# Score units in pairs of their own place, and two engines' SBUF operations ordered apart, in a decoder layer on one core

## Chip, cores, metric

One core of one Trainium2 chip. The metric is the device time of one launch in microseconds (us); lower is better. The kernel is one program with no loop on the chip: every engine has its own list of instructions, fixed when the kernel is built.

## What is computed

A decoder layer over `x` (4, 256, 256) in three sublayers, each followed by a residual sum and a layer norm over the last axis:

```python
x = _layernorm(x + attention(x, Wq, bq, Wk, bk, Wv, bv, Wo, bo))   # 32 query heads of 8, 8 key/value heads
x = _layernorm(x + wkv(w, u, x, ctx))                              # a decaying scan over the 256 steps
x = _layernorm(x + ffn(x))    # square(relu(x @ up)) @ down + (x @ expert) * (sum of the two largest gate logits),
                              # normalised with gamma and beta
```

## The kernel before

**Work and tiles.** The 4 batches of 256 rows are cut into 8 row tiles of 128. Attention calls a row tile s a *group* (0 to 7); the later sublayers call it a *chunk* p (0 to 7), and chunks 6 and 7 have some steps on VectorE that are GpSimd's or ScalarE's for the others.

**Score units.** Attention of one group is 16 units, 128 in all, and each has two halves. A *maxima unit* M n (`maxima_unit`, L600) is two matmuls of 256 columns into the bank `ps_max[n % 2]`; VectorE reduces the bank to row maxima (L1180). An *exp unit* E n (`exp_unit`, L613) is one matmul of 512 columns into `ps_exp[n % 2]`; ScalarE takes its exponential into `probs` (L812). Both work on 64 of the 128 rows of TensorE's array: `maxima_of` and `exp_unit` give each unit the upper or the lower half. M n waits until VectorE has reduced unit n - 2, E n until ScalarE has done unit n - 2. Four units' `probs` then go through `pv_group` (L629, 32-column matmuls, "pv"), four such groups per row tile. The maxima of half a group are split (`parts`), transposed (`m`, L692), copied (`mt`) and sent by a DMA of the SP queue (`mc`, L550) into the rows of `q_rows` that the exp units of that group read.

**Other TensorE steps.** They use all 128 rows: `k`, `q` (L665, L676), `op` (L722), `expert` (L747), `up` (L764, eight matmuls each), `down` (L781, four each), and the transposes `ht`, `att`, `x1`, `yt`, `x2` (L702, L712, L585, L734).

**Order.** The table `AT` gives every step of every group or chunk a tick, and each engine's builder walks the ticks and emits its own steps in that order; on one tick the score units come first. Score units have no entries of their own: unit n's maxima lie on tick `START + R * n` and its exponential on `START + R * (n + LAG)` with R = 32 and LAG = 15, so that TensorE's list always has E n, M n + 15 side by side. Engines wait for each other only through semaphores; an instruction behind a waiting one waits too. The SP queue issues nearly all DMAs, in the order of `AT`; ScalarE's queue issues some of the first batch (`kc1`, `kc2`, `qc01`, `qc02`). Before the first exp unit, TensorE also runs matmuls without use (`idle_matmul`, L635): sixteen ahead of M 0 and one behind each of M 0 to M 14. GpSimd clears the row buffers of batches 1 to 3 (L979 to L982) ahead of everything else that it does in the ticks.

Of the kernel before, what the change touches and what calls it, by code (L numbers as in the profile page):

```python
# [6 lines left out]
def decoder_layer(nc, x, x_cols, ctx_cols, w_qk, w_post, up_w, down_w, out):  # L7
# [42 lines left out]
    AT = {  # L50
        "k": (1456, 2315, 2440, 3400),
        "kv": (-1, 2342, 2463, 3423),
        "k1": (1514, 2367, 2505, 3466),
        "kr": (1542, 2381, 2625, 3501),
        "vc": (1610, -1, -1, -1),
        "k2": (1580, 2527, 3002, 3551),
        "k3": (1661, 2784, 3522, 3773),
        "q0": (1503, 2379, 2792, 3624),
        "qs0": (-1, 2399, 2875, 3647),
        "qh0": (1561, 2540, 2904, 3685),  # L60
        "qr0": (1589, 2556, 3075, 3742),
        "qm0": (1618, 2603, 3177, 4479),
        "ql0": (1643, 2641, 3398, 4558),
        "q1": (1561, 2536, 2920, 3560),
        "qs1": (-1, 2559, 2975, 3583),
        "qh1": (1803, 2716, 3023, 4019),
        "qr1": (1831, 2748, 3052, 4075),
        "qm1": (1860, 2801, 3092, 4264),
        "ql1": (1885, 2922, 3110, 4538),
        "kc0": (1542, 2381, 3240, 4435),  # L70
        "kc1": (1634, 2637, 3618, 4606),
        "kc2": (1703, 2805, 3852, 4658),
        "qc00": (1644, 2556, 3102, 4698),
        "qc01": (1771, 2697, 3344, 4508),
        "qc02": (1737, 2830, 3655, 4911),
        "qc10": (1831, 2869, 3550, 4417),
        "qc11": (1931, 2937, 3184, 4896),
        "qc12": (1989, 3087, 3963, 4919),
        "load": (2110, 2145, 2179, 2324, 2683, 2857, 3075, 3295, 3839, 3867, 3910, 3941, 3993, 4675),
# [1374 lines left out]
```

## Time and profile before

| | us |
|---|---|
| median of 3 runs | 216.71 (216.0 to 216.72) |
| profiled execution: span from first to last instruction | 215.5 |
| TensorE busy in the span | 199.6 |
| VectorE / ScalarE / GpSimd busy | 163.9 / 150.9 / 125.2 |
| mean granted TensorE clock, share of full speed | 0.991 |

The page has no time for the profiled execution other than its span. Busy time counts an instruction from its start to its end, and a matmul's end lies well behind the point at which the next one may start; so what a matmul costs is the distance from its start to the next start, where nothing waits.

### The profile page before, as it was taken

How to read it: one execution, taken by the hardware profiler on the slowest of the kernel's cores; microseconds unless marked ns; L12 is line 12 of the kernel's file. 1: busy time of each engine (PE TensorE's matmuls, PEld its weight loads, DVE VectorE, ACT ScalarE, POOL GpSimd, SP SyncE). 2: the span in 40 equal slices, each digit the busy share in tenths (PEclk: the TensorE clock that was granted, in tenths of full speed). 3: DMA queues.
4: the chain of work that ended last, by engine and by line, in shares of the span. 5: the costliest groups of instructions: out<-in, count | busy, mean ns of one | idle time of the engine just before them, and what ended most of it. 6: DMA issues, size and time to landing. Idle time of an engine off the chain costs nothing.

```text
span 215.5 us, 4364 instructions
## 1 busy us (share of the span) xinstructions
PE 199.6 (93%) x1295; PEld 111.8 (52%) x1295; DVE 163.9 (76%) x416; ACT 150.9 (70%) x334; POOL 125.2 (58%) x232
## 2 busy tenths in 40 slices
PE   7899999979999899999999999999999998799970
PEld 2533543433442344575465446655655487798950
DVE  3459787878899999998979899976754837956274
ACT  2310376857899779989799879998976985764520
POOL 8995164662554733467366776856485294177522
PEclk9999999999999999999999999999999999999996
DMA  4046226954015702131000000001000000000001
GB/s 122 26 124 179 70 54 217 251 132 115 20 52 151 269 3 62 43 96 30 25 6 5 8 0 9 2 24 33 2 6 0 3 24 26 0 5 2 34 15 49
DMA packets 14759, 12.35 MB, mean 57 GB/s; under 512 B 3856, under 2 KB 12688, under 8 KB 14480
## 3 DMA queue, kind: packets, MB, share of 16 engines
q1 hardware_dynamic: 14064, 11.72, 19.4%
q10 hardware_dynamic: 672, 0.36, 0.6%
q8 instruction: 10, 0.16, 0.3%
q14 instruction: 13, 0.11, 0.2%
HBM read 6.57 MB, written 1.05 MB: 35 GB/s over the span
## 4 chain that ended last, share of the span: by engine, by line
PE 75%; DMA 6%; ACT 6%; DVE 6%; issue 3%; ACTq 1%; POOL 0%; POOLq 0%; DVEq 0%
PE ps_b L764 12%; PE ps_heads L629 11%; PE ps_b L781 11%; PE ps_exp L613 10%; PE ps_max L600 6%; DMA q_rows<-max_t 4%; PE ps_exp L764 3%; PE ps_b L747 3%; PE ps_a L676 3%; PE ps_a L722 3%; ACT probs L812 2%; PE ps_a L665 2%; PE ps_exp L635 2%; DVE maxima L1180 2%; DMA qk_sb<-in_w_qk 2%
## 5 line engine op out<-in xcount | busy, mean ns | idle before, releaser
L1180 DVE TENSOR_REDUCE maxima<-ps_max 128x2 f32<-128x512 f32 x128 | 85.0, 684 | 10.4 <-PE ps_max L600 9.6
L812 ACT ACTIVATE probs<-ps_exp 128x512 f32<-128x512 f32 x128 | 73.6, 599 | 15.0 <-PE ps_exp L613 14.5
L613 PE MATMUL ps_exp<-q_rows,k_rows 64*128 64x512 bf16 x128 | 45.9, 385 | 4.0 <-DMA q_rows<-max_t 1.9
L600 PE MATMUL ps_max<-k_rows,q_rows 64*128 64x256 bf16 x256 | 47.2, 274 | 0.7 <-DMA q_rows<-q_parts 0.5
L1058 POOL TENSOR_TENSOR rstd<-var_eps,minus_half 128x1 f32<-128x1 f32 x32 | 19.4, 609 | 31.9 <-DVE var_eps L1151 31.7
L613 PEld LDWEIGHTS ps_exp<-q_rows,k_rows 64*128 64x128 bf16 x128 | 11.3, 93 | 44.7 <-ACT probs L812 25.5
L629 PE MATMUL ps_heads<-probs,v_cols 128*32 128x512 f32 x256 | 33.9, 604 | 0.0
L781 PE MATMUL ps_b<-down_sb,inner_t 128*128 128x256 f32 x112 | 29.4, 388 | 0.7 <-ACT relu_t L943 0.7
L764 PE MATMUL ps_b<-x_t,up_sb 128*128 128x128 f32 x192 | 27.1, 285 | 1.1 <-DVE h L1367 1.1
L764 PEld LDWEIGHTS ps_b<-x_t,up_sb 128*128 128x128 f32 x192 | 23.2, 191 | 6.0 <-issue 4.0
L781 PEld LDWEIGHTS ps_b<-down_sb,inner_t 128*128 128x128 f32 x112 | 19.4, 190 | 4.3 <-issue 1.5
L1142 DVE BATCH_NORM_STATS2 stats<-h 128x6 f32<-128x256 f32 x32 | 13.4, 422 | 7.4 <-POOL h L1126 7.0
L600 PEld LDWEIGHTS ps_max<-k_rows,q_rows 64*128 64x128 bf16 x256 | 14.7, 94 | 6.4 <-DVE maxima L1180 3.9
L1071 POOL TENSOR_TENSOR new_v<-wgt,ctx_t 128x256 f32<-128x256 f32 x14 | 10.4, 743 | 5.8 <-issue 4.5
L1037 POOL TENSOR_TENSOR maxima<-maxima 128x16 f32<-128x16 f32 x28 | 6.4, 228 | 10.2 <-DVE maxima L1180 8.9
L898 ACT ACTIVATE wgt<-delta,bonus_decay 128x128 f32<-128x128 f32 x32 | 10.9, 400 | 0.5 <-DVE delta L1276 0.5
L980 POOL MEMSET q_rows<- 128x4096 bf16 x3 | 10.5, 3512 | 0.0
L905 ACT ACTIVATE wgt<-wgt 128x512 f32<-128x512 f32 x16 | 10.2, 636 | 0.1
L949 ACT ACTIVATE inner_t<-relu_t 128x512 f32<-128x512 f32 x16 | 9.9, 628 | 0.1
L1087 POOL TENSOR_TENSOR y_num<-wgt,num 128x256 f32<-128x256 f32 x8 | 5.6, 698 | 7.0 <-DVE num L1305 7.0
L635 PE MATMUL ps_exp<-ident_bf 128*128 128x512 bf16 x31 | 9.5, 384 | 0.0
L943 ACT ACTIVATE relu_t<-ps_b 128x512 f32<-128x512 f32 x12 | 7.2, 597 | 2.6 <-PE ps_b L764 2.6
(129 smaller groups left out, 342.4 us busy)
## 6 DMA issues: line engine op xcount, KB each, us to landing
q_rows<-q_parts SPq DMA_DIRECT2D x46, 64.0 KB, 2.1
x_t<-in_x_cols SPq DMA_DIRECT2D x4, 256.0 KB, 3.5
x_in<-in_x SPq DMA_DIRECT2D x4, 256.0 KB, 4.6
ctx_t<-in_ctx_cols SPq DMA_DIRECT2D x4, 256.0 KB, 3.0
up_sb<-in_up_w SPq DMA_DIRECT2D x1, 1024.0 KB, 6.8
down_sb<-in_down_w SPq DMA_DIRECT2D x1, 1024.0 KB, 6.0
out_y<-y_out SPq DMA_DIRECT2D x8, 128.0 KB, 1.7
post_sb<-in_w_post SPq DMA_DIRECT2D x1, 906.0 KB, 5.3
```

The costliest lines, as they stand in the source:

```text
L600: last = nc.tensor.matmul(ps_max[n % 2][:, r, :], q_rows[b][at:at + HALF, g, REP * jj + 2 * half + r, h * P:h * P + P], k_rows[b][at:at + ...
L613: nc.tensor.matmul(ps_exp[n % 2][:, :], k_rows[b][at:at + HALF, JH * g + jj, kt * P:kt * P + P], q_rows[b][at:at + HALF, g, REP * jj:REP * ...
L629: last = nc.tensor.matmul(ps_heads[s % 2][32 * j:32 * j + 32, :], flat(v_cols[b][:, :, :])[:, at:at + 32], probs[(4 * n + j) % 8][:, :], s ...
L635: nc.tensor.matmul(ps_exp[1][:, :], src[:, 0:P], src[:, 0:P].rearrange("p (a t) -> p a t", a=1) .broadcast_to([P, REP, P]), start=True, st ...
L764: last = nc.tensor.matmul(ffn_banks[k][:, v * n:v * n + n], up_sb[:, c, m * P:m * P + P], x2_t[:, c, columns_of(p)], start=(c == 0), stop= ...
L781: last = nc.tensor.matmul(down_part(p, i), inner_t[:, m, i * P:i * P + P], down_sb[:, m, :], start=(m == 0), stop=(m == NI - 1))
L812: nc.scalar.activation(probs[n % 8][:, :], ps_exp[n % 2][:, :], ACT.Exp, scale=SCALE).then_inc(s_exp, 1)
L898: last = nc.scalar.activation(wgt[:, 2 + i, c, cols], delta[:, c, cols], ACT.Relu, scale=sign, bias=bonus_decay[:, i, c:c + 1])
L980: gp.memset(q_rows[b][:], 0.0).then_inc(s_ones, 1)
L1058: gp.tensor_tensor(rstd[k][:, ti], var_eps[k][:, ti], minus_half[:, ti], ALU.pow).then_inc(s_rstd[k], 1)
L1142: own(nc.vector.bn_stats(stats[k][:, i, :], src[:, i, :]))
L1180: nc.vector.tensor_reduce(maxima[s % 2][:, g, j // JH, 0, at:at + 2], ps_max[n % 2][:, :, :], AX, ALU.max, negate=True).then_inc(s_max, 1)
```

## The change

`R`, `START` and `LAG` go. Score units get lists in `AT`: `score_max` and `score_exp` (TensorE), `max` (VectorE), `exp` (ScalarE), 128 places each. The whole table is written anew as places 0 to 1366, so the order of steps changes on every queue, GpSimd's and SP's too. The memsets of GpSimd get places among its other steps, the idle matmuls get the lists `warm` and `idle`, and `hn` waits for the `hn` before it. `maxima_of` keeps the number 15 under the name `PAIRING`, so each unit keeps its half of the array.

```diff
-    R = 32
-    START = 1920
-    LAG = 15
+    PAIRING = 15
     AT = {
-        "k": (1456, 2315, 2440, 3400),
-        "load": (2110, 2145, 2179, 2324, 2683, 2857, 3075, 3295, 3839, 3867, 3910, 3941, 3993, 4675),
-        "mc0": (2311, 2785, 3329, 3804, 4393, 4880, 5290, 5906),
-        "mc1": (2534, 3055, 3532, 4102, 4591, 5104, 5640, 6183),
-        "up0": (4648, 5096, 5736, 5860, 6481, 6843, 7370, 7974),
-        "yt": (4399, 4900, 5368, 5543, 6121, 6383, 7103, 7700),
+        "load": (1, 53, 54, 120, 141, 267, 268, 289, 579, 580, 581, 826, 919, 929),
+        "k": (2, 15, 138, 313),
+        "clear_q": (-1, 13, 61, 273),
+        "warm": (20, 21, 25, 30, 32, 33, 34, 35, 36, 37, 40, 41, 42, 43, 44, 48),
+        "score_max": (50, 55, 59, 66, 70, 73, 75, 78, 82, 86, 89, 94, 98, 100, 105, 108, 118, 119, 135, 136, 145,
...
+        "idle": (51, 58, 65, 67, 72, 74, 76, 79, 85, 88, 93, 96, 99, 101),
+        "mc0": (102, 199, 293, 440, 560, 741, 841, 994),
+        "score_exp": (103, 111, 114, 116, 125, 142, 153, 160, 161, 166, 175, 182, 183, 189, 197, 204, 211, 212, 222,
...
+        "mc1": (132, 249, 384, 481, 642, 773, 959, 1074),
+        "yt": (490, 648, 816, 912, 1107, 1163, 1223, 1297),
+        "up0": (578, 727, 914, 954, 1178, 1204, 1244, 1318),
...
@@ tensor
-                n = unit_of(tick, exp_tick(0))
+                n = SCORE_EXP.get(tick)
                 if n is not None:
                     exp_unit(n // UNITS, n % UNITS)
-                n = unit_of(tick, max_tick(0))
+                n = SCORE_MAX.get(tick)
                 if n is not None:
...
                     maxima_unit(n // UNITS, n % UNITS)
-                    if n < LAG:
+                for k in range(WARM_ROWS):
+                    if AT["warm"][k] == tick:
+                        if k < 2:
+                            pe.wait_ge(s_q2[0], 1)
+                        elif k < WARM_ROWS - 2:
+                            pe.wait_ge(s_q3[0], 1)
+                        else:
+                            pe.wait_ge(s_krows[0], 16 * len(BLOCKS))
                         idle_matmul(ident_bf)
+                if tick in AT["idle"]:
+                    idle_matmul(ident_bf)
@@ scalar
-                n = unit_of(tick, exp_tick(0))
+                n = EXP_OF.get(tick)
@@ gpsimd
+                for b in range(1, B):
+                    if AT["clear_k"][b] == tick:
+                        gp.memset(k_rows[b][:], 1.0).then_inc(s_ones, 1)
...
@@ vector
-                n = unit_of(tick, max_tick(0))
+                n = MAX_OF.get(tick)
...
                         dve.wait_ge(s_headst, s + 1)
+                        if s >= 1:
+                            dve.wait_ge(s_att, s)
```

Sorted by tick, the same stretch of TensorE's list reads (steps as name.chunk or name.group; E and M are units):

```
before  E83 M98 ht.4 m1.5 E84 M99 up0.1 E85 M100 up1.1 E86 M101 att.4 E87 M102 pv0.5 E88 M103 op.4 E89 M104
after   E83 m1.5 up2.1 ht.4 up3.1 M99 E84 E85 M100 att.4 pv0.5 M101 E86 E87 M102 op.4 M103 E88 down1_0.1 yt.2 M104 E89 E90 M105
```

A *run* below is a stretch of E and M with no other step between. Counted so from E 0 to the end of the list, before has 103 runs, after 73; from E 0 to E 63 it is 42 and 38, from E 64 to E 127 it is 60 and 34, and one behind. Steps that change the kind of matmul (64-row score unit, 32-column pv, 128-row step): 210 before, 159 after.

## Rows read from the trace of the kernel before

**Rows 1.** The page: span, and busy time of each engine.
```profile
span 215.5 us, 4364 instructions
PE 199.6 (93%) x1295; PEld 111.8 (52%) x1295; DVE 163.9 (76%) x416; ACT 150.9 (70%) x334; POOL 125.2 (58%) x232
```
**Rows 2.** Busy time by stretch: E 0 to 31, 63, 95, 127, last matmul, end.
```profile
core 0: us, PE busy (x) PEld busy (x) DVE busy (x) ACT busy (x) POOL busy (x), PEclk, DMA share, GB/s
25.40:52.10 26.70, 24.49 (x185) 10.29 (x184) 21.40 (x42) 19.36 (x40) 13.11 (x31) 1.00 0.54 144
52.10:81.20 29.10, 27.13 (x197) 11.09 (x193) 26.51 (x53) 25.53 (x58) 15.16 (x32) 1.00 0.35 105
81.20:123.60 42.40, 42.31 (x301) 23.46 (x301) 38.42 (x98) 38.02 (x89) 25.62 (x47) 1.00 0.13 35
123.60:170.40 46.80, 46.67 (x297) 25.55 (x296) 35.17 (x103) 40.49 (x94) 29.66 (x54) 1.00 0.03 9
170.40:208.60 38.20, 36.34 (x239) 31.41 (x235) 23.54 (x83) 23.19 (x48) 21.48 (x38) 1.00 0.05 15
```
**Rows 3.** The chain that ended last, in order of time: start us, us, what.
```profile
42.21 4.14 DMA q_rows<-max_t
...
71.72 3.61 DMA q_rows<-max_t
...
95.30 0.87 PE ps_a L722 x4
96.17 0.89 PE ps_b L764 x8
...
103.22 1.00 PE ps_heads L629 x8
104.54 1.06 PE ps_b L781 x4
...
109.85 1.09 PE ps_b L764 x8
...
112.67 0.37 PE ps_a L712 x2
...
170.45 0.32 PE ps_exp L613
...
174.38 0.22 PE ps_a L585 x2
...
189.69 1.78 PE ps_exp L764 x16
...
194.31 1.73 PE ps_b L781 x8
```
**Rows 4.** Timeline of TensorE's matmuls: start us, us, what (two exp units in one run).
```profile
60.40 0.39 PE L613 MATMUL ps_exp<-q_rows,k_rows 64*128 64x512 bf16 x1
60.63 0.38 PE L613 MATMUL ps_exp<-q_rows,k_rows 64*128 64x512 bf16 x1
```
**Rows 5.** The same, cut at 29.899 us, and then whole.
```profile
29.67 0.39 PE L613 MATMUL ps_exp<-q_rows,k_rows 64*128 64x512 bf16 x1
29.68 0.49 PE L600 MATMUL ps_max<-k_rows,q_rows 64*128 64x256 bf16 x3
...
29.90 0.38 PE L613 MATMUL ps_exp<-q_rows,k_rows 64*128 64x512 bf16 x1
```
**Rows 6.** Costliest groups by line: busy us, mean ns, idle before.
```profile
L1180 DVE TENSOR_REDUCE maxima<-ps_max 128x2 f32<-128x512 f32 x128 | 85.0, 684 | 10.4 <-PE ps_max L600 9.6
L600 PE MATMUL ps_max<-k_rows,q_rows 64*128 64x256 bf16 x256 | 47.2, 274 | 0.7 <-DMA q_rows<-q_parts 0.5
...
L980 POOL MEMSET q_rows<- 128x4096 bf16 x3 | 10.5, 3512 | 0.0
```
**Rows 7.** DMA issues by line: KB each, median us to landing.
```profile
x_t<-in_x_cols SPq DMA_DIRECT2D x4, 256.0 KB, 3.5
x_in<-in_x SPq DMA_DIRECT2D x4, 256.0 KB, 4.6
...
up_sb<-in_up_w SPq DMA_DIRECT2D x1, 1024.0 KB, 6.8
down_sb<-in_down_w SPq DMA_DIRECT2D x1, 1024.0 KB, 6.0
```
**Rows 8.** Start-up: ScalarE's work and its DMA issues, and the chain up to M 0.
```profile
8.84 0.42 ACT L853 ACTIVATE q_parts<-q_rest 128x256 bf16<-128x256 f32 x1 [0.25 <-DVE q_rest L1194]
8.90 2.07 ACTq L495 DMA_DIRECT2D k_rows<-k_parts  x3
11.07 1.22 ACTq L489 DMA_DIRECT2D q_rows<-q_parts  x2
...
11.72 2.02 DMA q_rows<-q_parts
13.88 0.38 PE ps_max L600 x2
```
**Rows 9.** Start-up: SP's DMA of the first maxima, and TensorE ahead of E 0.
```profile
22.00 0.54 SPq L550 DMA_DIRECT2D q_rows<-max_t  x1
...
24.42 1.03 PE L676 MATMUL ps_a<-x_t,qk_sb 128*128 128x256 f32 x4
```
**Rows 10.** One step of VectorE: duration min/median/max ns, first and last start.
```profile
L1358 DVE TENSOR_TENSOR route<-top x8: 159/160/647, 88.5 to 202.2; 128x1 f32<-128x1 f32 x8
```

More of the change, by code:

```diff
@@ L43, in decoder_layer @@
     WIDE = sum(b < B - 1 for b, tiles in CHUNKS)
-    R = 32
-    START = 1920
-    LAG = 15
+    PAIRING = 15
     AT = {
-        "k": (1456, 2315, 2440, 3400),
[L52 to L78, printed above, removed]
-        "load": (2110, 2145, 2179, 2324, 2683, 2857, 3075, 3295, 3839, 3867, 3910, 3941, 3993, 4675),
[17 rows of a table removed]
-        "att": (3119, 3916, 4333, 4751, 5167, 5656, 6186, 6734),
-        "att_e": (3135, 4030, 4319, 4735, 5182, 5662, 6175, 6760),
-        "xbo": (2985, 3148, 3697, 4454, 5032, 5129, 5552, 6707),
[30 rows of a table removed]
-        "unit": (4161, 4847, 5263, 5482, 6055, 6279, 6991, 7521),
-        "raw": (4205, 4821, 5299, 5464, 6078, 6262, 6940, 7596),
[42 rows of a table removed]
-        "store": (5888, 6047, 6548, 7059, 7989, 8247, 8651, 8825),
@@ new lines, in decoder_layer @@
+        "load": (1, 53, 54, 120, 141, 267, 268, 289, 579, 580, 581, 826, 919, 929),
+        "k": (2, 15, 138, 313),
+        "k1": (3, 19, 147, 360),
+        "kr": (4, 22, 319, 365),
+        "vc": (5, -1, -1, -1),
+        "q0": (6, 45, 165, 381),
+        "k2": (7, 109, 352, 366),
+        "k3": (8, 122, 353, 502),
+        "qh0": (9, 63, 311, 434),
+        "kc2": (10, 134, 428, 676),
+        "q1": (11, 155, 206, 342),
+        "clear_k": (-1, 12, 60, 158),
+        "clear_q": (-1, 13, 61, 273),
@@ new lines, in decoder_layer @@
+        "kc0": (14, 92, 408, 588),
+        "qr0": (16, 64, 359, 435),
+        "qm0": (17, 113, 361, 515),
+        "kv": (-1, 18, 139, 314),
+        "warm": (20, 21, 25, 30, 32, 33, 34, 35, 36, 37, 40, 41, 42, 43, 44, 48),
+        "kc1": (23, 144, 427, 746),
+        "ql0": (24, 143, 362, 522),
+        "qc01": (26, 186, 429, 546),
+        "qc00": (27, 152, 312, 673),
+        "qc02": (28, 181, 410, 701),
+        "qh1": (29, 157, 279, 542),
+        "qc10": (31, 239, 303, 657),
+        "qr1": (38, 190, 284, 543),
@@ new lines, in decoder_layer @@
+        "qm1": (39, 208, 288, 584),
+        "ql1": (46, 209, 299, 670),
+        "qc11": (47, 215, 310, 659),
+        "clear_v": (-1, 49, 151, 274),
+        "score_max": (50, 55, 59, 66, 70, 73, 75, 78, 82, 86, 89, 94, 98, 100, 105, 108, 118, 119, 135, 136, 145,
[6 rows of a table added]
+        "idle": (51, 58, 65, 67, 72, 74, 76, 79, 85, 88, 93, 96, 99, 101),
+        "qc12": (52, 248, 462, 671),
+        "max": (56, 57, 68, 69, 71, 77, 80, 81, 83, 87, 95, 97, 104, 106, 110, 117, 128, 129, 137, 140, 148, 149,
[11 rows of a table added]
+        "score_exp": (103, 111, 114, 116, 125, 142, 153, 160, 161, 166, 175, 182, 183, 189, 197, 204, 211, 212, 222,
[6 rows of a table added]
@@ new lines, in decoder_layer @@
+        "exp": (107, 115, 123, 124, 126, 150, 154, 162, 163, 176, 178, 187, 188, 196, 198, 205, 213, 216, 226, 235,
[20 rows of a table added]
+        "att": (246, 394, 548, 604, 784, 958, 1082, 1191),
+        "att_e": (255, 409, 562, 605, 795, 967, 1090, 1194),
+        "op": (264, 438, 563, 627, 800, 968, 1091, 1202),
+        "start": (276,),
+        "xbo": (277, 285, 331, 592, 738, 747, 922, 1211),
[28 rows of a table added]
+        "unit": (455, 631, 799, 908, 1083, 1157, 1216, 1284),
+        "yn1": (476, 624, 804, 909, 1059, 1154, 1213, 1278),
@@ L175, in decoder_layer @@
+        "raw": (477, 644, 805, 910, 1081, 1161, 1215, 1289),
[42 rows of a table added]
+        "store": (1131, 1146, 1210, 1340, 1357, 1358, 1360, 1366),
     }
     WARM = 8
-    ROW_FILL = 2
+    WARM_ROWS = 16
     TICKS = range(max(max(v) for v in AT.values()) + 1)
@@ L185, in decoder_layer @@
     NP = len(PARCELS)
-    def max_tick(n):
-        return START + R * n
-    def exp_tick(n):
-        return START + R * (n + LAG)
-    def unit_of(tick, first):
-        n, rest = divmod(tick - first, R)
-        return n if rest == 0 and 0 <= n < UNITS * GROUPS else None
+    SCORE_MAX, SCORE_EXP, MAX_OF, EXP_OF = ({tick: n for n, tick in enumerate(AT[name])}
+                                            for name in ("score_max", "score_exp", "max", "exp"))
     def before(p, batches=1):
@@ L410, in maxima_of @@
         def maxima_of(i):
-            tile = 1 - (i - LAG) % 4 // JH
-            k = sum(1 - (m - LAG) % 4 // JH == tile for m in range(i))
+            tile = 1 - (i - PAIRING) % 4 // JH
+            k = sum(1 - (m - PAIRING) % 4 // JH == tile for m in range(i))
             return k // 4, JH * tile + k // 2 % 2, k % 2
@@ L642, in _ @@
             for tick in TICKS:
-                n = unit_of(tick, exp_tick(0))
+                n = SCORE_EXP.get(tick)
                 if n is not None:
                     exp_unit(n // UNITS, n % UNITS)
-                n = unit_of(tick, max_tick(0))
+                n = SCORE_MAX.get(tick)
                 if n is not None:
-                    if n == 0:
-                        for done, value, n_idle in ((s_q2[0], 1, ROW_FILL), (s_q3[0], 1, 6 * ROW_FILL),
-                                                    (s_krows[0], 16 * len(BLOCKS), ROW_FILL)):
-                            pe.wait_ge(done, value)
-                            for k in range(n_idle):
-                                idle_matmul(ident_bf)
-                    maxima_unit(n // UNITS, n % UNITS)
-                    if n < LAG:
+                    maxima_unit(n // UNITS, n % UNITS)
+                for k in range(WARM_ROWS):
[6 more added lines that the diff above has]
+                            pe.wait_ge(s_krows[0], 16 * len(BLOCKS))
                         idle_matmul(ident_bf)
+                if tick in AT["idle"]:
+                    idle_matmul(ident_bf)
                 for b in range(B):
@@ L977, in _ @@
             gp.memset(heads_of(v_cols[0])[:, :, :, HD:HD + 1], 1.0).then_inc(s_const, 1)
-            for b in range(1, B):
-                gp.memset(k_rows[b][:], 1.0).then_inc(s_ones, 1)
-                gp.memset(q_rows[b][:], 0.0).then_inc(s_ones, 1)
-                own(gp.memset(v_cols[b][:], 0.0))
-                gp.memset(heads_of(v_cols[b])[:, :, :, HD:HD + 1], 1.0).then_inc(s_const, 1)
-            gp.memset(minus_half[:], -0.5).then_inc(s_const, 1)
-            gp.memset(top[:, :, 0:1], NEG).then_inc(s_const, 1)
-            gp.memset(num[:, :, 0:1], 0.0).then_inc(s_const, 1)
-            gp.memset(den[:, :, 0:1], 0.0).then_inc(s_const, 1)
             def bonus():
@@ L995, in _ @@
             for tick in TICKS:
+                for b in range(1, B):
+                    if AT["clear_k"][b] == tick:
+                        gp.memset(k_rows[b][:], 1.0).then_inc(s_ones, 1)
+                    if AT["clear_q"][b] == tick:
+                        gp.memset(q_rows[b][:], 0.0).then_inc(s_ones, 1)
+                    if AT["clear_v"][b] == tick:
+                        own(gp.memset(v_cols[b][:], 0.0))
+                        gp.memset(heads_of(v_cols[b])[:, :, :, HD:HD + 1], 1.0).then_inc(s_const, 1)
+                if AT["start"][0] == tick:
+                    gp.memset(minus_half[:], -0.5).then_inc(s_const, 1)
+                    gp.memset(top[:, :, 0:1], NEG).then_inc(s_const, 1)
+                    gp.memset(num[:, :, 0:1], 0.0).then_inc(s_const, 1)
+                    gp.memset(den[:, :, 0:1], 0.0).then_inc(s_const, 1)
                 for b in range(1, B):
```

194 rows, old and new, of the table AT are left out of this document.

## The prediction

> **What bounds it.** I read the page for the share of each engine, then busy time by stretch with the edges at E 0, E 63, E 127 and the last matmul, then the chain that ended last, whose pieces give what a TensorE step costs when nothing waits. TensorE is busy 199.6 of 215.5 us [rows 1], but that share hides three stages [rows 2]. Stage A (25.4 to 81.2, 55.8 us) has attention and little else: TensorE has gaps, and in its second half VectorE is busy 26.5 of 29.1. Stage B (81.2 to 170.4, 89.2 us) has attention beside the feed-forward: TensorE 42.31 of 42.40 and 46.67 of 46.80, ScalarE 78.5 and VectorE 73.6 of the 89.2. Stage C (38.2 us) is feed-forward alone, and 6.9 us of VectorE and GpSimd end it. The clock is granted in full in all of them, so no time hangs on it.
>
> What fills TensorE in B is partly not work. The chain [rows 3] shows eight `up` matmuls in 0.89 us behind another 128-row step, and in 1.09 behind a score unit; four `down` in 0.87 (1.73 for eight) and in 1.06; two transposes in 0.22 and in 0.37. So a 128-row step behind another kind of matmul pays 0.20 (transposes 0.15). And a score slot (E with an M beside it) alone takes 0.32 where slots in one run follow at 0.23 [rows 4]: leaving a run costs 0.09 more. A change of kind therefore costs about 0.095; the other 0.105 of the 0.20 (0.055 for transposes) is paid once per block of 128-row steps, at its second matmul.
>
> **The sum, TensorE.** Both tables, sorted, give the lists; I price each list without waits: 0.216 us per 256-column matmul (1.73 / 8), 0.111 per `up` (1.78 / 16), 0.109 per transpose (0.22 / 2), a pv group 0.90 (1.00 less a change of kind), 0.23 per score slot, or, in a run, per unit of whichever array half has more, and the changes. Before comes to 48.1 (A), 88.9 (B), 35.1 (C) against 55.8, 89.2, 38.2 measured: 7.7, 0.3 and 3.1 us are waits. So B is TensorE's list and nothing else.
> - Removed: 210 - 159 = 51 changes of kind x 0.095 = 4.8 us. Blocks of several 128-row matmuls that begin behind another kind go from 64 to 39: 25 x about 0.105 = 2.6. Together 7.4 us, nearly all in B, where runs go from 60 to 34 (in A 42 to 38, since there E n, M n + 15 mostly touch already).
> - Unchanged: the matmuls themselves. In both lists the larger half of the array summed over all runs is 128 units, so pairs cost no streaming if the halves overlap as they do now.
> - Moved: one pv group (0.9) and about 1.2 of score units go from B to A, and 1.1 of feed-forward from B to C.
> The new list is 48.9, 79.6 and 36.2: 0.8 more, 9.3 less, 1.1 more.
>
> **What the pairs wait for.** Two units at once want both banks. Behind M n comes a 0.68 us reduce [rows 6]; a run with M n and M n + 1 must find both done or TensorE stands. In A 21 runs already hold two M, in the new list 29; in B 2 become 22, but a slot pair there has 79.6 / 32 = 2.5 us for two reduces (1.37) and two exponentials. The fuller engines are the limit: steps worth 4 of ScalarE's 94 us by their listed durations leave B, so of its 78.5 busy us about 75 remain; VectorE has about 74, against a list of 79.6. ScalarE had 10.7 us idle there; it would have 4 if TensorE never waited. Nothing in the trace shows this closer fit; by its bounds the new waits in B are 0.3 (as now) or 6.4 (ScalarE keeps all its idle time). I take 4.4, towards the upper end, since 95% on two engines with one queue each rarely fits. B: 84.0, which is 5.2 less.
>
> **Stage A.** Two waits in the chain are DMAs of maxima, 4.14 us at 42.2 and 3.61 at 71.7 [rows 3], each issued behind a bulk load of 1 MB (`up`, `down`), which takes 6 to 7 us to land [rows 7]. The new SP order puts the transfer at 42.2 (`mc1.1`) ahead of `up`, but then `up`, `x_t` 3 and `x_in` 1, 1.5 MB, ahead of `mc0.2`; `down` goes behind `mc0.4`, 5 us or more ahead of its first reader. Both of these waits should shrink, and VectorE, 91% busy, takes the place. I take 6.7 of 7.7 us of waits: A is 55.6, 0.2 less.
>
> **Start.** M 0 waits for ScalarE's five DMA issues, 8.90 to 12.29, the last landing 2.02 later [rows 8]. The new order puts on ScalarE `k2` ahead of `qh0`, a `k3` wait and `kv.1` (0.47) among them: M 0 some 0.8 us later, about 14.7. But `k.1` and `q0.1` (0.86 each) now run in that hole; `q0.1` stood straight ahead of E 0 [rows 9]. The maxima DMA went out 8.1 us behind M 0; the new list has `m0.0` one slot (0.64) earlier: about 7.4, so at 22.1. Landing takes 2 us: E 0 near 24.4 for 25.4. I take 1.0 gained; bounds are 0.8 lost (M 0 decides) and 1.5 gained. GpSimd's memsets, 3.5 us each for the query rows [rows 6], are moved out of the way of `k1.1`; that is worth nothing, since `kv.1` is later than they are.
>
> **Stage C** has 36.2 of list. Its waits were 3.1. From `x1.6` to `yt.6` the old list has 18.9 us of other work, the new only 13.3, and the scan chain with ScalarE's share needs about 12.5 by my count: I take 3.5, so 39.7, 1.5 more. The last 6.9 us stay; their steps and order are the same.
>
> **VectorE apart from GpSimd.** A 0.16 us sum takes up to 0.65 beside GpSimd [rows 10]. There are nine such stretched steps, some 2.5 us in all, most hidden under a full TensorE. Priced at nothing; if that cover goes, 1 us of gain. The `hn` wait is on work long done: nothing.
>
> Sum: -1.0 - 0.2 - 5.2 + 1.5 = -4.9 us. The profiled span of 215.5 becomes 210.6; the median of the runs shown stands 1.2 above that span, so 216.7 becomes 211.8.
>
> **Rivals.**
> *The halves don't overlap in the new patterns.* Today E and M alternate on opposite halves; M beside M is nowhere in the trace. If every matmul had to start behind the one before it in the program, M n, with its second matmul 0.12 behind its first, would hold up its neighbour, and score streaming after E 0 would grow by 6.2 us: a gain of 1.2 of list, less in waits: 216.5. Against it: by 29.899 us three maxima matmuls have started, and the exp matmul that stands ahead of the third in the list starts at 29.90 [rows 5]; a step for the free half passes a blocked one. The Trainium skill says the opposite (TensorE: Matmul & The Clock Gate, part 3 on packing): matmuls start and end strictly in program order. By that rule this rival's 216.5 would be the forecast; the trace disagrees, in one pattern.
> *ScalarE takes over.* It keeps its 10.7 us of idle time in B: B is 86, total 213.8; with a longer C chain (from `x1.6`, 2 us) up to 215.8.
> *Slower: both banks at once.* TensorE is in order, so a run placed early blocks all behind it. 28 runs newly hold two M. If each waits for half a reduce (0.34 us), that is 9.5 us: 221.3. It decides from 0.17 us a run. For it: VectorE already waits 9.6 us for maxima [rows 6], and the new order fixes places with no regard to what is ready. Against it: 2.5 us per pair in B, and the waits in A with runs of two M are mostly DMAs.
>
> **How the numbers follow.** A run of this kernel can tell 0.5% (about 1.1 us) from no change. Forecast 0.60, ScalarE and chain 0.15, halves 0.10, both banks 0.15. The forecast's own range is 208.0 to 214.3 (waits in B 0.3 to 6.4, start -1.5 to +0.8, the VectorE gain). With ScalarE's case and the halves' the range is 207.5 to 217. Faster by over 0.5% (below 215.6): the forecast and most of the second case, 0.74; within: 0.12; slower (above 217.8): 0.14.
>
> **What would show it.** Right: TensorE starts fall about 7 us shorter between E 0 and the last matmul, `up` pieces at 0.89 outnumber those at 1.09, a run of M M E E takes about 0.46 us, ScalarE over 90% busy in B. Wrong: such a run takes 0.57 or more; TensorE waits on maxima or `probs` inside runs in B; `yt.6` late in C. The forecast fails if B isn't at least 3 us shorter.

## The result, and the profile after

Before 216.72 us (median of four runs, 216.0 to 217.08), after 209.26 (208.51 to 209.47): ratio 0.967 with a 95% interval of 0.964 to 0.971, so 7.5 us faster. The forecast was 211.8. The profiled execution of after has a span of 207.4 and a time of 209.23, 1.8 us more; that same 1.8 stands between span and time in every run here, so the profiled execution of before (215.5) was one of about 217.3, 0.6 above its median. The spans differ by 8.1 us.

The page of after: span and busy time (those of before are [rows 1]), then the engines' shares of its chain of work that ended last:

```profile
span 207.4 us, 4363 instructions
PE 193.4 (93%) x1294; PEld 111.7 (54%) x1294; DVE 169.9 (82%) x416; ACT 150.9 (73%) x334; POOL 126.8 (61%) x232
...
PE 53%; DVE 15%; issue 9%; POOL 8%; ACT 7%; SPq 3%; DMA 2%; ACTq 0%; POOLq 0%; DVEq 0%
```

TensorE is as full as before, by share. VectorE is busy 6.0 us longer for the same steps, which the change was said to spare. Busy time by stretch, with the edges at E 0, E 63, E 127 and the last group of `down` matmuls, which starts at 199.44 (columns as in [rows 2]; the edge of the rows lies 0.16 behind that start):

```profile
0.00:23.02 23.02, 21.46 (x87) 9.54 (x88) 13.96 (x27) 4.67 (x9) 16.13 (x26) 1.00 0.40 113
23.02:76.39 53.37, 52.10 (x380) 21.11 (x379) 48.80 (x99) 44.61 (x96) 32.64 (x69) 1.00 0.33 94
76.39:160.52 84.13, 81.22 (x590) 48.74 (x587) 74.82 (x188) 75.80 (x174) 51.43 (x94) 1.00 0.16 47
160.52:199.60 39.08, 37.71 (x242) 31.87 (x239) 28.79 (x95) 25.46 (x56) 25.32 (x43) 1.00 0.04 12
```

Beside the stages of before (edges there 25.38, 81.19, 170.38, 207.52) and those of a run of before's order in the new code, shown further down, the forecast reads:

| part | forecast | after, less profiled before | after, less before's order in the new code |
|---|---|---|---|
| up to E 0 | -1.0 | -2.4 | -1.5 |
| stage A | -0.2 | -2.4 | -2.3 |
| stage B | -5.2 | -5.1 | -5.0 |
| stage C | +1.5 | +1.8 | +1.8 |
| end | 0 | 0 | 0 |
| sum | -4.9 | -8.1 | -7.1 |

Four score units on two banks and both halves, TensorE's matmuls in after (columns as in [rows 4]):

```profile
133.82 0.39 PE L636 MATMUL ps_exp<-q_rows,k_rows 64*128 64x512 bf16 x1 [0.36 <-DMA q_rows<-max_t]
133.83 0.39 PE L623 MATMUL ps_max<-k_rows,q_rows 64*128 64x256 bf16 x2
134.05 0.38 PE L636 MATMUL ps_exp<-q_rows,k_rows 64*128 64x512 bf16 x1
134.06 0.38 PE L623 MATMUL ps_max<-k_rows,q_rows 64*128 64x256 bf16 x2
134.37 0.48 PE L747 MATMUL ps_a<-post_sb,att_t 128*128 128x256 f32 x1
```

From the first score unit to the next 128-row step it is 0.55 us: two slots of 0.23 and one change of kind. M beside M on opposite halves occurs as well: the first matmuls of M 52 and M 53 start at 55.282 and 55.288, the second ones at 55.402 and 55.409, and it is 0.326 us to the next kind, what a single slot takes. The pairs cost no streaming. Of the 32 `up` pieces, counted from start to the next matmul's, 11 of before took 0.9 us, 10 took 1.0 and 10 took 1.1; in after 18 take 0.9 and one takes 1.1.

### The profile page after: what moved, and what is told of

Its sections match the earlier page's. It is cut to its first block, busy times and chain, and to the rows that moved or that the text cites. A ratio compares the mean times of both kernels' runs of the same rounds, so it can differ in the third digit from the quotient of the medians.

```text
span 207.4 us, 4363 instructions
## 1 busy us (share of the span) xinstructions
PE 193.4 (93%) x1294; PEld 111.7 (54%) x1294; DVE 169.9 (82%) x416; ACT 150.9 (73%) x334; POOL 126.8 (61%) x232
## 4 chain that ended last, share of the span: by engine, by line
PE 53%; DVE 15%; issue 9%; POOL 8%; ACT 7%; SPq 3%; DMA 2%; ACTq 0%; POOLq 0%; DVEq 0%
PE ps_heads L652 8%; PE ps_b L806 8%; PE ps_max L623 7%; PE ps_exp L658 6%; PE ps_exp L636 5%; DVE maxima L1209 4%; PE ps_exp L789 3%; PE ps_b L789 3%; ACT probs L837 3%; PE ps_a L701 2%; DMA q_rows<-max_t 2%; PE ps_a L747 2%; SPq L518 2%; PE ps_b L772 2%; PE ps_a L690 2%
## 5 line engine op out<-in xcount | busy, mean ns | idle before, releaser
L1209 DVE TENSOR_REDUCE maxima<-ps_max 128x2 f32<-128x512 f32 x128 | 82.3, 681 | 8.2 <-PE ps_max L623 7.8
L837 ACT ACTIVATE probs<-ps_exp 128x512 f32<-128x512 f32 x128 | 71.4, 598 | 15.8 <-PE ps_exp L636 15.2
L623 PE MATMUL ps_max<-k_rows,q_rows 64*128 64x256 bf16 x256 | 41.9, 273 | 1.9 <-DVE maxima L1209 1.7
L636 PE MATMUL ps_exp<-q_rows,k_rows 64*128 64x512 bf16 x128 | 39.4, 383 | 1.2 <-DMA q_rows<-max_t 0.6
L623 PEld LDWEIGHTS ps_max<-k_rows,q_rows 64*128 64x128 bf16 x256 | 15.2, 94 | 28.4 <-DVE maxima L1209 23.0
L806 PE MATMUL ps_b<-down_sb,inner_t 128*128 128x256 f32 x112 | 27.1, 384 | 0.2
L789 PE MATMUL ps_b<-x_t,up_sb 128*128 128x128 f32 x192 | 24.4, 277 | 0.3 <-DVE h L1398 0.2
L806 PEld LDWEIGHTS ps_b<-down_sb,inner_t 128*128 128x128 f32 x112 | 20.0, 190 | 3.5 <-issue 0.7
L636 PEld LDWEIGHTS ps_exp<-q_rows,k_rows 64*128 64x128 bf16 x128 | 9.8, 93 | 17.6 <-ACT probs L837 13.6
L1100 POOL TENSOR_TENSOR new_v<-wgt,ctx_t 128x256 f32<-128x256 f32 x14 | 10.7, 766 | 8.6 <-issue 5.4
L1066 POOL TENSOR_TENSOR maxima<-maxima 128x16 f32<-128x16 f32 x28 | 6.4, 230 | 14.1 <-DVE maxima L1209 12.9
L815 ACT ACTIVATE x_t<-ps_a 128x256 f32<-128x256 f32 x16 | 6.1, 384 | 4.6 <-PE ps_a L608 4.5
```

Of the source, the lines that this page charges most:

```text
L623: last = nc.tensor.matmul(ps_max[n % 2][:, r, :], q_rows[b][at:at + HALF, g, REP * jj + 2 * half + r, h * P:h * P + P], k_rows[b][at:at + ...
L636: nc.tensor.matmul(ps_exp[n % 2][:, :], k_rows[b][at:at + HALF, JH * g + jj, kt * P:kt * P + P], q_rows[b][at:at + HALF, g, REP * jj:REP * ...
L789: last = nc.tensor.matmul(ffn_banks[k][:, v * n:v * n + n], up_sb[:, c, m * P:m * P + P], x2_t[:, c, columns_of(p)], start=(c == 0), stop= ...
L806: last = nc.tensor.matmul(down_part(p, i), inner_t[:, m, i * P:i * P + P], down_sb[:, m, :], start=(m == 0), stop=(m == NI - 1))
L837: nc.scalar.activation(probs[n % 8][:, :], ps_exp[n % 2][:, :], ACT.Exp, scale=SCALE).then_inc(s_exp, 1)
L1100: gp.tensor_tensor(new_v[:, half, :, cols], wgt[:, 1 + 2 * half, :, cols], ctx_t[b][:, :, cols], ALU.mult).then_inc(s_newv[half], 1)
```

## The experiments

Every engine of the new code takes its steps in the order of a table. Most kernels here are the new code with other tables: one engine's list changed, or all lists cut at one place and joined to the other order. Times are medians; each was timed beside runs of before, to which the ratios refer.

**Before's order in the new code.** It separates order and code.

```diff
 # all five engines
-order: the new places
+order: the places of before, GpSimd's memsets first
```

> Edit: the code of after (tables of places, warm-up split in two places, GpSimd's memsets as steps, the extra wait ahead of the copy into the heads) with every engine's steps in before's order. Theory 1 (the order alone makes the difference): 0.5% or less from before. Theory 2 (the code, such as the warm-up's waits or the k.0 that started at 4.28 instead of 4.97 with the old start, is worth something): 0.7 to 1.5 us faster, with M 0 near 12.3 instead of 13.9.

Measured 216.49 us beside 216.68, ratio 1.002 (0.999 to 1.005). The code alone is worth nothing, and this run is a second trace of before's order:

```profile
0.00:24.53 24.53, 22.07 (x94) 9.90 (x94) 15.26 (x29) 4.30 (x8) 18.93 (x30) 1.00 0.39 112
24.53:80.21 55.68, 51.76 (x376) 21.33 (x377) 47.92 (x94) 44.83 (x98) 28.20 (x62) 1.00 0.43 123
80.21:169.38 89.17, 88.93 (x594) 49.00 (x594) 73.55 (x200) 78.42 (x182) 55.15 (x101) 1.00 0.08 21
169.38:206.70 37.32, 35.52 (x236) 31.06 (x233) 23.34 (x83) 23.17 (x48) 20.76 (x37) 1.00 0.05 16
```

From the start of the last group (206.51) back, the stages are those of before within 0.2 us: 55.7, 89.2, 37.1. Only the start differs, E 0 at 24.53 instead of 25.38: `k.0` began at 4.43 instead of 4.97, and its four matmuls took 1.43 us instead of 1.78. So 0.85 of the 2.4 us that the two first profiles showed for the start lie ahead of M 0 and are not the order's. Four more traces of the new code with this start, of runs further down (loads, pairs twice, old order up to E 64), have E 0 at 23.89 to 24.23, and `k.0` at 4.32 to 4.43. There is one trace of the old code, so it isn't shown whether its late `k.0` is scatter or the code's; the times (216.49 beside 216.68) show no difference.

**The start alone.** Twice: once cut just ahead of E 0, and once a little behind, since the first had a seam.

```diff
 # TensorE around E 0, first cut; the rest in before's order
-... M13 E0 M14 M15 E1 v.0 E2 ...
+... M13 v.0 M14 E0 M15 E1 ...
 # second cut
+... M13 E0 M14 M15 E1 v.0 E2 E3 M16 M17 | k.2 M18 m1.0 ...
```

> Edit: the kernel before, but every engine does the steps that come ahead of E 0 in the new order (TensorE, ScalarE, VectorE, GpSimd and the DMA queue alike); from E 0 on each engine keeps its old order. The slots are then the old ones. E 0 should start near 23.0 us (it is 25.4 before and 23.0 after). Theory 1, the start is worth what it shows at E 0, and the parts add up: 2.4 us faster than before, 214.3 (span 213.1). Theory 2, stage A is held by VectorE and by the DMAs of maxima and gives it back: E 63 no more than 1 us earlier than 81.2, the total 215.7 or more.

> Edit: the new order on every engine up to the place of VectorE's first copy of v (TensorE up to M 17), the old order behind it; the run with the new start alone had a seam, in which v.0 stood ahead of M 14 and cost 1.5 us. E 0 near 23.0, where the old order in the new code has 24.5. Theory 1 (the start's gain goes through to the end): 1.2 to 1.6 us faster than before. Theory 2 (it is given back at the next wait of stage A, a DMA of rows or of maxima, whose issue does not depend on E 0): within 0.5 us of before at E 31 and at the end. Theory 3 (it is worth more than E 0 shows, as the run with the old start and the rest new lost 2.9 us to after): 2.5 us or more faster.

The first: 219.34 beside 216.06, ratio 1.015 (1.011 to 1.018), slower. `v.0` stands ahead of M 14 there, and from M 10 to E 0 it takes 4.4 us instead of the 2.8 of after; E 0 is at 24.9. Its profiled execution (217.42) was the fastest of six and has the span of before; in the others the mean granted clock was 0.975 to 0.987 instead of 0.990. Where they lost it no trace shows. That the new start by itself slows the kernel does not follow from it. The second: 217.0 beside 216.47, ratio 1.002 (1.000 to 1.005). Its E 0 is at 23.07, as in after, and nothing of it reaches the end. That is theory 2's number for the end, but its reason isn't shown: E 31 comes at 53.76 in this trace, 2.6 us later than in before's order. The profiled execution is 1.7 us above the median span of its kernel (215.1); in it TensorE's granted clock fell behind a short stretch of gaps:

```profile
23.00:25.00 2.00, 1.78 (x12) 0.83 (x12) 1.83 (x4) 1.16 (x2) 0.61 (x6) 1.00 0.54 131
25.00:27.00 2.00, 1.49 (x8) 1.06 (x7) 1.75 (x5) 0.00 (x0) 0.00 (x0) 0.80 0.01 4
27.00:29.00 2.00, 1.77 (x7) 0.40 (x7) 0.35 (x2) 1.20 (x3) 0.52 (x2) 0.50 0.00 0
29.00:31.00 2.00, 2.00 (x7) 1.17 (x4) 1.17 (x2) 0.84 (x2) 1.16 (x2) 0.50 0.17 40
31.00:33.00 2.00, 1.96 (x13) 1.06 (x11) 0.95 (x2) 1.47 (x3) 0.00 (x0) 0.50 0.35 92
33.00:35.00 2.00, 2.00 (x23) 0.73 (x24) 1.45 (x4) 1.05 (x3) 0.00 (x0) 0.99 0.55 114
```

(Stretches of 2 us; the column behind POOL is the clock.) `k.2` waits for its input at 25.9, the clock is at its lower level (1.2 GHz) until 33, and from E 0 to E 7 it takes 9.6 us where before's order takes 5.4 and after 6.9. Four of its twelve executions, the profiled one among them, have a mean granted clock of 0.971 to 0.978 and took 218.6 to 221.2 us; the other eight, at 0.989 to 0.996, took 216.3 to 217.3. So even with the clock kept the earlier E 0 gains nothing.

**The old start with the rest new.**

```diff
 # all engines: before's order ahead of E 0, then the new places
-... M13 idle E0 M14 M15 E1 v.0 E2 ...
+... M12 idle k.1 q0.1 M13 E0 M14 M15 E1 E2 ...
```

> Edit: the kernel after, but the steps ahead of E 0 in the old order on every engine, and the rest in the new one. E 0 should start near 25.4. Theory 1 (parts add up): 2.4 us slower than after, 211.7. Theory 2 (stage A has slack that only a DMA or VectorE fills): 210.3 or less.

Measured 212.15 beside 216.06, ratio 0.980 (0.978 to 0.983) where after has 0.967: 2.9 us lost. E 0 came at 23.61, 0.6 later than in after, but E 15 at 39.13 for 35.90: the projections of the second batch, that the new stage A counts on, were late, and the clock was at 0.67 from 27 to 29 us and at 0.5 from 29 to 31. So the new start is worth up to 2.9 us, to the new stage A alone, and part of that is the clock, which this run doesn't separate; in before's order it is worth nothing.

**The stages apart.** All engines cut at E 64.

```diff
 # first: new up to E 64, before's order behind it
+... E62 M75 E63 m0.4 expert0.0 M76 M77 att.2 pv3.3 M78 M79 v.2 v.3 op.2 | E64 ht.3 ...
 # second: before's order up to E 64, new behind it
+... E63 M78 pv2.3 pv3.3 op.2 x2.0 expert0.0 M79 | E64 E65 M80 M81 E66 ht.3 ...
```

> Edit: every engine keeps the new order for all steps that stand ahead of E 64 in it, and the old order for what is left: start and stage A new, B and C old. Theory 1 (each stage has its own gain): E 64 at 76 to 77 us instead of 81 to 82, B takes its old 89 us (its list, full of changes of kind), C its old 37 to 38: 4.8 us faster than before, 211.9. Theory 2 (the gain of A is work pushed into B): B grows by about what A gained, 215 or more.

> Edit: the other half of the same cut: the old order for what stands ahead of E 64 in it, the new order for what is left: start and stage A old, B and C new. Theory 1: E 64 at 81 to 82 as before, B 84 us and C 39 as after: 3.3 us faster than before, 213.4. Theory 2 (A's gain is pushed work, B's gain comes in full): B is the shorter by the 0.9 us pv group that is not pushed, 212 to 213. Theory 3 (B needs the state that the new A leaves, such as which maxima and exponentials are done ahead): B gains less than 3 us, 215 or more.

First 214.53 beside 216.06, 0.992 (0.990 to 0.995): -1.5 us. Second 216.08, 0.999 (0.996 to 1.001): 0. The halves together make 1.5 us, the whole makes 7.5. In the first, start and A keep all of their gain, B is 2.6 us longer than in before's order, and C is the same:

```profile
0.00:23.31 23.31, 21.75 (x88) 9.84 (x88) 13.97 (x27) 4.67 (x9) 16.13 (x26) 1.00 0.38 111
23.31:76.65 53.34, 52.06 (x380) 21.09 (x379) 48.84 (x99) 44.61 (x96) 32.61 (x69) 1.00 0.32 94
76.65:168.39 91.74, 90.22 (x596) 49.58 (x594) 74.55 (x200) 78.48 (x182) 54.14 (x99) 1.00 0.14 43
168.39:205.50 37.11, 35.31 (x235) 30.86 (x232) 23.17 (x82) 23.17 (x48) 20.77 (x37) 1.00 0.05 16
```

In the second, E 79 to E 127 takes 60.6 us as in after (61.0; before's order 67.5): B's gain is there. But E 63 to E 79 takes 27.0 for 23.1 (before's order 21.6), with gaps behind the cut (3.83 of the first 5.5 us busy) and the clock at 0.72 from 86 to 92 us. So theory 1 of both holds for the stages themselves and fails at the seams, where steps that one order has done and the other counts on are missing.

**The bulk loads behind the maxima.** Of before's DMA queue alone:

```diff
-... qc02.1 up qc10.1 qc11.1 mc1.1 x_t3 qc12.1 ...
+... qc02.1 qc10.1 qc11.1 mc1.1 up x_t3 qc12.1 ...
-... down x_in2 ctx2 qc12.2 x_in3 mc1.3 mc0.4 ...
+... qc12.2 mc1.3 down x_in2 ctx2 x_in3 mc0.4 ...
```

> Edit: before's order, only the DMA queue's changed: the 1 MB up load goes behind the copy of maxima mc1.1, and down, x_in 2, ctx 2 and x_in 3 go behind mc1.3. The two waits of 1.43 us (at 42.2) and 0.73 us (at 71.7) for those copies should be gone. Theory 1 (these two DMA waits are what stage A gained beyond its list): E 63 1.5 to 2.2 us earlier than before, total 1.5 to 2.2 us less. Theory 2 (VectorE, 91% busy there, holds A): E 63 at most 0.7 us earlier, total within 0.5% of before.

Measured 220.35 beside 216.68, 1.020 (1.016 to 1.023): slower, which neither theory had. The waits of TensorE's weight loads from 40 to 60 us, first in before's order, then here (engine, what waited, for what: us in total, times, longest):

```profile
PEld ps_exp L646 <- ACT probs L848: 5.3, 10, 0.8
PEld ps_exp L646 <- DMA q_rows<-max_t: 1.4, 1, 1.4
```

```profile
PEld ps_max L1283 <- DMA q_rows<-q_parts: 5.1, 1, 5.1
PEld ps_exp L1296 <- ACT probs L1498: 3.9, 7, 1.0
```

The wait for the maxima is gone, and one of 5.1 us for the query rows of the second batch stands in its place. In the chain it is their last copy, `qc12.1`:

```profile
42.94 7.66 DMA q_rows<-q_parts
```

That copy is behind `up` and `x_t` 3 in both orders. But in before's order `up` went out at 36.17 and had landed at 43.12, so the copy, issued at 42.74, landed at 46.45; here `up` goes out at 41.60, 1.3 us ahead of the copy, which lands at 50.60. Behind the wait the clock is at 0.50 until 55 us, so a part of the loss is the clock's. To move `up` back needs those copies done first, as in after, where the DMA queue has the last six of them ahead of the second maxima (start us, us, what):

```profile
34.91 0.53 SPq L573 DMA_DIRECT2D q_rows<-max_t  x1
35.55 3.76 SPq L512 DMA_DIRECT2D q_rows<-q_parts  x6
40.73 0.53 SPq L573 DMA_DIRECT2D q_rows<-max_t  x1
41.31 0.59 SPq L541 DMA_DIRECT2D up_sb<-in_up_w  x1
```

For that `k.1` and `q0.1` run early in after, and GpSimd's memsets mostly behind the first parts of the second batch: its first cast of `k_parts` starts at 9.7 us in after and at 23.9 in before.

**Pairs on TensorE alone, and on three engines.** Before's order, from E 64 on:

```diff
 # TensorE (both runs), for even n from 64 on
-E80 M95 down0_3.0 x2.1 E81 M96 pv3.4
+E80 M95 E81 M96 down0_3.0 x2.1 pv3.4
 # second run also: ScalarE, VectorE
+exp80 exp81 ...    max95 max96 ...
```

> Edit: before's order, only TensorE's changed, and only from E 64 on: for even n from 64 to 124 (118 left out) E n+1 and M n+16 are brought up to stand right behind slot n, ahead of the feed-forward or pv steps that stood between. TensorE's runs of score units after E 0 go from 103 to 76, changes of kind from 210 to 168, blocks of 128-row steps from 64 to 49. Its list gets shorter by 42 x 0.095 + 15 x about 0.105, with rounding 5.2 us. Theory 1 (the list binds B, changes of kind are the price): 3.5 to 5.2 us faster, B 84 to 86 us. Theory 2 (both banks at once: VectorE and ScalarE keep their old order, so the second unit of a pair waits for its bank): the waits on maxima and probs inside runs eat it, from 1 us faster to 4 us slower.

> Edit: as the run with pairs on TensorE alone, but the matching steps go along: where E n+1 and M n+16 are brought up behind slot n (even n from 64 to 124, 118 now too), ScalarE's exp n+1 goes right behind exp n and VectorE's reduce n+16 right behind n+15. TensorE's list is 5.3 us shorter than before's (changes of kind 210 to 167, blocks 64 to 49). Theory 1 (changes of kind bind B, and the run before lost only because ScalarE's and VectorE's old order made the second unit wait): 3 to 5.3 us faster than before, 211 to 213.5, and its B stage 84 to 86 us. Theory 2 (two slots back to back need both banks free, and no order of the others helps): slower than before or within 1 us. Theory 3 (the matched places of all other steps are what the new order brings, pairs alone are half of it): 1 to 3 us faster.

TensorE alone: 223.17 beside 216.68, 1.031 (1.027 to 1.034), 6.5 us slower with 5.2 us less of list. Even theory 2 was too mild. TensorE's matmuls and ScalarE's steps at 105 us show one place of it:

```profile
105.51 0.39 PE L808 MATMUL ps_exp<-q_rows,k_rows 64*128 64x512 bf16 x1
105.52 0.39 PE L795 MATMUL ps_max<-k_rows,q_rows 64*128 64x256 bf16 x2
106.66 0.39 PE L808 MATMUL ps_exp<-q_rows,k_rows 64*128 64x512 bf16 x1 [0.76 <-ACT probs L1010]
```

```profile
105.53 0.60 ACT L992 ACTIVATE x<-h,offset,rstd 128x256 f32<-128x256 f32 x1 [0.73 <-POOL offset L1266]
106.03 1.65 ACT L1010 ACTIVATE probs<-ps_exp 128x512 f32<-128x512 f32 x3
```

E 81 needs the bank that exponential 79 reads. ScalarE begins it at 106.03, 4.5 us after E 79 (101.57): the normalisation `nor1.1` stands ahead of it in ScalarE's queue, that waits for GpSimd's offset, and so for `yt.1`, which TensorE's new list has behind E 79 and M 94, at 102.20 instead of 99.53 (1.7 of these 2.7 us were lost ahead of E 78 already). With exponentials and reduces moved along: 215.11 beside 216.47, 0.993 (0.991 to 0.996), 1.4 us faster. The two differ by 8 us with nearly the same TensorE list: what the other engines do in between decides. B is 87.5 in it, a list about 5.3 shorter than before's with about 3.6 us of new waits. That is theory 3's number, at its lower end: pairs alone are a part. That the fitted places of all other steps are the rest is inferred, not shown by a run.

**Splitting the runs of after.** On TensorE alone:

```diff
-E2 E3 M16 M17 E4 m1.0 pv0.0 M18 ...
+E2 E3 M16 m1.0 M17 E4 pv0.0 M18 ...
```

> Edit: the kernel after, only TensorE's order changed: in 41 runs of four or more score units the last two go behind the next other step. Runs after E 0 go from 73 to 90, changes of kind from 159 to 187, blocks from 39 to 50; the list gets longer by 28 x 0.095 + 11 x 0.105, with rounding 4.1 us. Theory 1 (changes of kind set the time, waits absorb part of it): 2 to 4 us slower than after (211 to 213). Theory 2 (after is held by VectorE, ScalarE and waits, TensorE has room): within 1 us of after.

Measured 224.58 beside 216.68, 1.038 (1.034 to 1.042): 15 us above after for 4.1 us of list. Two thirds of it are there by E 63 (86.7 for 76.4), where its waits are for `probs` 10.7 us and for maxima 9.4, where after has 5.3 and 12.8, with pv groups and projections (`q_rest`) now waiting too. The clock fell as well: behind 2 us in which TensorE was busy 1.50 it is at 0.50 from 26 to 32 us, and E 0 to E 7 takes 10.4 us for 6.9. This run can't weigh the list's price; it shows again that one engine's list can't be moved alone.

**Without columns shared by GpSimd and VectorE.** GpSimd's 256-column steps of the scan and the feed-forward are left out and a memset and a power on one column stand in for each.

```diff
-gp.tensor_tensor(new_v[:, half, :, cols], wgt[...], ctx_t[...], ALU.mult)
+gp.memset(filler[:, at:at + 1], 1.0)
+gp.tensor_tensor(new_v[:, half, 0, 0:1], unit_col[:], unit_col[:], ALU.pow)
```

> Edit: the kernel after, with GpSimd's 256-column operations of the feed-forward and the scan (x + bias, new_v, y_den, y_num, their products with 1/y, x2 + beta, gamma and beta) each replaced by a memset and a power on one column, about 0.70 us together against 0.75; these results are left out, the waits stay. VectorE's stretched steps beside them should go: its busy time from 169.9 to 162 or less. Theory 1 (the stretching is hidden under TensorE): the time within 1 us of after. Theory 2 (it is paid, since VectorE holds TensorE's banks): 3 us or more faster than after, most of it in stage B.

> Edit: as the run before without shared columns, which lost 4.4 us between E 15 and E 31 to the seven memsets that it had put on GpSimd ahead of the first x + bias. Now the first two chunks (four for x2 + beta) keep their 256-column operations, so no tile has to be filled, and the replacement by a memset and a power on one column begins with chunk 2; those results are left out. Up to E 79 it is after, 99.5. Theory 1 (VectorE's stretching is hidden under TensorE): within 1 us of after, and what the run before gained from E 31 on was only work that its late stage A had left. Theory 2 (it is paid): E 79 to the last matmul 3 us or more shorter than the 100.0 of after, total 3 us or more below after.

The first: 208.29 beside 216.47, 0.962 (0.961 to 0.964), 1.1 us below after; but the memsets that it added to GpSimd held up the residual of `op.0` in stage A, and TensorE's next use of that bank waits 3.7 us. The second has no such fill: 204.22 beside 216.32, 0.945 (0.943 to 0.947) where after has 0.967, **4.9 us below after**. Up to E 79 it is after, and E 79 comes at 99.30 for 99.49. Its stages, and two groups of VectorE, first of this run, then of after (columns as in [rows 6]):

```profile
76.19:156.73 80.54, 80.25 (x590) 48.77 (x588) 70.04 (x188) 74.92 (x174) 47.02 (x131) 1.00 0.17 49
156.73:194.50 37.77, 36.97 (x243) 31.97 (x240) 25.74 (x94) 25.19 (x56) 22.18 (x61) 1.00 0.04 12
...
L1320 DVE SCALAR_TENSOR_TENSOR delta<-top,post_sb,x_t 128x128 f32<-128x128 f32 x16 | 5.5, 363 | 0.4
...
L1402 DVE TENSOR_TENSOR route<-top 128x1 f32<-128x1 f32 x8 | 1.8, 225 | 0.3
```

```profile
L1307 DVE SCALAR_TENSOR_TENSOR delta<-top,post_sb,x_t 128x128 f32<-128x128 f32 x16 | 7.5, 488 | 0.4
...
L1389 DVE TENSOR_TENSOR route<-top 128x1 f32<-128x1 f32 x8 | 2.9, 356 | 0.3
```

VectorE's busy time falls from 169.9 to 162.5 us. Stage B comes to 80.5 us, where TensorE's new list without waits was priced at 79.6, and C to 37.6 for 38.9. From E 79 to the last matmuls it takes 95.0 us for 100.0: theory 2's numbers. The traces show the stretching step by step. Of VectorE's 72 steps of the kinds scan, `delta` and `route`, those that took over 1.3 times the lower quartile of their group are 8 in before (2.3 us above it in all), 25 in after (8.6 us) and 7 in this run (2.3 us), and each of these 7 lies beside a 256-column step of GpSimd that was left. One place in after shows how, with VectorE, GpSimd and TensorE in turn:

```profile
121.45 1.55 DVE L1298 TENSOR_TENSOR_SCAN top<-post_sb,x_t 128x128 f32<-128x128 f32 x2
123.03 1.44 DVE L1307 SCALAR_TENSOR_TENSOR delta<-top,post_sb,x_t 128x128 f32<-128x128 f32 x2
...
124.73 0.67 DVE L1209 TENSOR_REDUCE maxima<-ps_max 128x2 f32<-128x512 f32 x1
```

```profile
121.86 0.85 POOL L1119 TENSOR_TENSOR y_num<-y_num,new_v 128x256 f32<-128x256 f32 x1
122.86 0.73 POOL L1129 TENSOR_TENSOR y_num<-y_num,y_inv 128x256 f32<-128x256 f32 x1
123.55 0.78 POOL L1082 TENSOR_TENSOR h<-x_in,post_sb 128x256 f32<-128x256 f32 x1
```

```profile
125.46 0.28 PE L623 MATMUL ps_max<-k_rows,q_rows 64*128 64x256 bf16 x1 [1.37 <-DVE maxima L1209]
```

The same two scans and two deltas take 0.94 and 0.61 in the run without shared columns, and M 114 does not wait there. What this run can't separate: each stand-in takes about 0.67 us (0.10 and 0.57) for the 0.75 of the step that it replaces, so GpSimd's part of the chain got shorter too, by some 4.5 us of busy time over 56 steps. The 4.9 us are therefore what both are worth together, and an upper bound for the stretching alone.

## Why the prediction was right, and where it was not

- **TensorE's list in B, right.** Before 88.9 of 89.2 us was the forecast's reading, a new list of 79.6 its price. With the disturbance of VectorE taken away B is 80.5. So the list priced at 0.095 per change of kind and 0.105 per block of 128-row steps comes within 0.9 us of a whole stage. It is no proof of each price: what waits are left in these 80.5 us was not taken apart.
- **New waits in B, right in size by luck, wrong in cause.** Forecast 4.4, measured 84.1 - 79.6 = 4.5. The reason given was two engines at 95% with one queue each. But 3.6 of the 4.5 go when GpSimd's shared columns go. The failing step is "VectorE apart from GpSimd. Priced at nothing; if that cover goes, 1 us of gain". The trace of after has more stretched steps, not fewer: the deltas mean 488 ns for 352 in before, `num` 575 to 622 for 410 to 468, and VectorE's busy time is 6.0 us up. Whatever the new order keeps apart by its own reckoning, on the chip the scan meets GpSimd more often than before (25 stretched steps for 8), and it cost up to 4.9 us. With engines this full the cover was gone: what was bounded at 1 us of gain is a loss of up to several.
- **Stage A, mis-sized.** Forecast 6.7 us of waits on a list of 48.9, measured 53.4 - 48.9 = 4.5. The step that failed is "VectorE, 91% busy, takes the place". That share was of the second half alone; over A VectorE was busy 47.9 of 55.7 us, and in after is at 48.8 of 53.4, so there was room. In A TensorE's weight loads wait 0.7 us for DMAs of maxima, where before's order has 3.2, which the forecast had seen. What made it possible was missed: the loads moved alone cost 3.7 us, since the query copies of the next batch come behind them; in after these are ahead of both, and GpSimd's memsets are out of the way of those parts. How much of A's gain this is no run shows by itself. The forecast had priced the memsets at nothing "since `kv.1` is later than they are"; in the new order `kv.1` is not: it runs at 9.2 us.
- **Start, right but for its size.** M 0 was to come 0.8 later for ScalarE's new order: 13.79 against 13.03 in before's order in the new code, 0.76. Over all traces of the new code but the two cut just ahead of E 0 it is 1.1: 13.2 to 14.1 in six with the new start, 12.4 to 13.0 in five with before's. From M 0 to E 0 it takes 9.22 to 9.23 in those six and 11.50 in those five and in before, where the forecast had 9.7. Net that is -1.2 for -1.0; the rest of the -2.4 in the profiles lies ahead of M 0. What the forecast lacked is that a saving at E 0 is worth nothing by itself, as the second run with the new start shows, and up to 2.9 us to the stage behind it that needs its projections.
- **Stage C, right in size, in part for another reason.** Forecast +1.5 (1.1 of work that B no longer does, 0.4 of waits), measured +1.8, with TensorE waiting for the scan chain ahead of `yt` at 172.18 (0.26) and ahead of `x2` at 175.85 (0.17). But in the last run, with the same TensorE list, C is only 0.4 above before: 1.4 of the 1.8 go with GpSimd's shared columns.
- **The range.** The bounds that the forecast names (new waits in B, start, VectorE's gain) add up to 206.2 to 215.6; the 208.0 to 214.3 on record is narrower, and its working isn't given. The measured 209.26 lies in both.
- **The rivals.** *Halves don't overlap* falls: two slots in 0.45 us, M beside M as well. The Trainium skill (TensorE: Matmul & The Clock Gate, part 3 on packing) has matmuls start strictly in program order; the trace of after disagrees, as that of before did: M 53's first matmul (55.288) starts ahead of M 52's second (55.402), which stands before it in the list. *ScalarE takes over* falls: it idles 8.3 us in B (84.13 - 75.80). *Both banks at once* is what the trace shows when TensorE's list is moved alone (6.5 us slower in before, 15 in after, there with a fall of the clock) and cost little in a change that places the steps of all engines anew: TensorE's weight loads wait more often for maxima (44 times, 23.0 us) and less for `probs` (13.6 us for 25.5), mostly while it still streams: it is busy 81.2 of B's 84.1 us.

What stays open: how the 7.5 us divide between pairs and fitted places. The halves cut at E 64 add up to 1.5 us, pairs with matching exponentials to 1.4, the start to nothing, and every cut has a seam of its own. Not tried is a version of after that computes everything and keeps the scan's VectorE steps clear of GpSimd's; the last run puts the bound of its gain at 4.9 us.

## What to carry to other kernels

Price a reordering by the list of the engine that binds, and then look at which other queues stand behind its steps: one engine's list moved alone lost 7 us here for a list that was 5 shorter, and 15 for one that was 4 longer (some 4 of them with the clock), because in-order engines wait for each other crosswise. Where the engines beside the binding one are as full as here (VectorE 74.8 and ScalarE 75.8 of B's 84.1 us), an operation stretched by a neighbour may no longer be hidden, so count stretched steps (maximum against median of one line) in the new trace before believing that a change has removed them. A bulk load moved from ahead of one small transfer stands ahead of another: list what is behind it at its new place.
